# A two-layer decoder with a top-1 expert stage on one core: no fill of unused rows, five full expert blocks taken first, last logits from rows turned on TensorE, addresses loaded in groups

## What is computed

```python
x = x + local_attention(layernorm(x))                  # window of 257
x = x + perceiver_attention(ctx, layernorm(x))         # 8 heads of 128, keys = 1024 context + 512 own
x = x + bit_linear_ffn(layernorm(x))                   # int8 rows, ternary weights, conv, silu
x = x + self_attention_16_heads(layernorm(x))
x = x + rope_cross_attention_16_heads(layernorm(x), ctx)
# expert stage, over all B*S = 2048 rows
xf = layernorm(x); e = argmax(softmax(xf @ Wg + bg))   # one of NE = 8 experts per row
x = x + (gelu(xf @ W1[e] + b1[e]) @ W2[e] + b2[e])
```

## Time and profile before

| what | value |
|---|---|
| median of three runs | 2154.18 us |
| the profiled execution's own time | 2155.8 us |
| its span, first to last instruction | 2154.1 us |
| TensorE matmul busy | 1856.0 us (86%) |
| VectorE busy | 1631.2 us (76%) |
| ScalarE busy | 1281.1 us (59%) |
| GpSimd busy | 218.6 us (10%) |
| mean granted TensorE clock | 0.961 |

### The profile page before, as it was taken

How to read it: one execution, slowest core, us unless ns; L and a number is a source line. 1 busy time by engine, 2 the same in 40 slices (tenths; PEclk the granted TensorE clock), 3 DMA queues, 4 the chain that set the end, 5 groups by cost and what they waited for, 6 DMA issues and landing times.

```text
span 2154.1 us, 41917 instructions
## 1 busy us (share of the span) xinstructions
PE 1856.0 (86%) x17110; PEld 1031.9 (48%) x17110; DVE 1631.2 (76%) x2621; ACT 1281.1 (59%) x1919; POOL 218.6 (10%) x230
## 2 busy tenths in 40 slices
PE   4999988988999988988899978989899987468947
PEld 2576752324666652423666653323567663023224
DVE  8888878796888878696888768697778878339643
ACT  5666646487566656487566645668566645346912
POOL 1000001300100001300100001020100002003413
PEclk8999999999999999999999999999999999689978
DMA  7477710011477730010367640000277761942034
GB/s 273 74 126 118 133 50 12 9 46 31 82 123 126 125 65 12 9 45 21 79 121 124 115 91 12 9 26 21 62 123 124 124 117 30 127 64 101 2 88 107
DMA packets 454607, 169.51 MB, mean 79 GB/s; under 512 B 428389, under 2 KB 444016, under 8 KB 453904
## 3 DMA queue, kind: packets, MB, share of 16 engines
q1 hardware_dynamic: 449216, 149.29, 34.7%
q0 software_dynamic: 5200, 17.55, 4.9%
HBM read 45.14 MB, written 18.52 MB: 30 GB/s over the span
## 4 chain that ended last, share of the span: by engine, by line
PE 48%; DVE 27%; DMA 12%; ACT 6%; issue 4%; SPq 2%; POOL 1%; POOLq 0%; DVEq 0%; ACTq 0%
DVE nmx L2177 14%; DMA arena<-arena 11%; PE ps L753 8%; PE ps L755 8%; PE ps L754 7%; PE ps L1135 6%; PE ps L1121 3%; PE ps L925 3%; DVE arena L1987 3%; PE ps L919 2%; PE ps L920 2%; PE ps L1085 1%; ACT arena L1497 1%; PE ps L1145 1%; SPq L597 1%
## 5 line engine op out<-in xcount | busy, mean ns | idle before, releaser
L2177 DVE TENSOR_REDUCE nmx<-ps 128x2 f32<-128x1024 f32 x384 | 445.1, 1218 | 51.6 <-PE ps L1085 49.8
L1669 ACT ACTIVATE arena<-ps 128x512 f32<-128x512 f32 x768 | 406.8, 601 | 99.9 <-PE ps L1121 94.9
L1972 DVE TENSOR_SCALAR_CACHE_REDUCE ps<-ps 128x1536 f32<-128x1536 f32 x128 | 225.7, 1763 | 46.4 <-PE ps L755 45.6
L1135 PE MATMUL ps<-arena 128*17 128x256 f32 x3072 | 242.8, 393 | 0.0
L1987 DVE SCALAR_TENSOR_TENSOR arena<-arena,rs 128x1536 f16<-128x1536 f32 x128 | 231.6, 1809 | 4.2 <-ACT arena L1559 4.2
L1559 ACT ACTIVATE arena<-arena,rs 128x1536 f16<-128x1536 f32 x128 | 200.8, 1569 | 42.9 <-DVE rs L1978 42.9
L1121 PE MATMUL ps<-arena 64*128 64x512 f16 x768 | 171.0, 396 | 47.7 <-DMA arena<-arena 45.8
L1550 ACT ACTIVATE arena<-ps,nm 128x1536 f32<-128x1536 f32 x128 | 197.0, 1539 | 15.7 <-DVE ps L1972 15.7
L753 PE MATMUL ps<-arena 128*128 128x512 f16 (+2 forms) x508 | 178.5, 352 | 24.7 <-DMA arena<-zx_d 22.6
L919 PE MATMUL ps<-arena 128*128 128x128 f16 x1536 | 185.3, 219 | 0.8 <-DMA arena<-arena 0.8
L920 PE MATMUL ps<-arena 128*128 128x128 f16 x1536 | 185.3, 219 | 0.0
(11 more groups left out here) (334 smaller groups left out, 3553.7 us busy)
## 6 DMA issues: line engine op xcount, KB each, us to landing
zx_d<-in_eye POOLq DMA_DIRECT2D x7, 1300.0 KB
arena<-in_weights SPq DMA_DIRECT2D x8, 929.0 KB, 18.2
arena<-arena SPq DMA_DIRECT2D x72, 64.0 KB, 2.1
arena<-arena SPq DMA_TRANSPOSE x272, 3.7
arena<-in_ctx SPq DMA_DIRECT2D x4, 1024.0 KB, 5.5
arena<-in_ctx_t SPq DMA_DIRECT2D x4, 1024.0 KB, 4.9
arena<-in_experts SPq DMA_DIRECT2D x1, 3840.0 KB, 11.5
arena<-zx_d SPq DMA_DIRECT2D x23, 132.0 KB, 2.2
```

The costliest lines, as they stand in the source:

```text
L1135: mm(ps[32 * j:32 * j + VW, 7, cols], v17[:, kt, 4 * g_ + j, :], pr_[:, (4 * t + j) % RING, cols], start=(kt + half == 0), stop=(kt == mod ...
L1669: A(pr_[:, n % RING, :], ps[:, 4 + n % 3, :], ACT.Exp).then_inc(b_exp.sem, 1)
L1972: TS_(s_, s_, -XS, None, ALU.mult, ALU.min, accum_out=nm[:, i:i + 1]).then_inc(s_max.sem, 1)
L2177: V.tensor_reduce(nmx[:, g_ % 2, ch, :, pp, i], ps[:, 2 * (z % 2):2 * (z % 2) + 2, :], AX.X, ALU.max, negate=True)\
```

## The change

- **No fill.** `pad_regions` and its eight DMAs go. A region now is `B*S + P` = 2176 rows and begins with 128 rows of a number out of bounds, written once at the start: SyncE issues eight DMAs of 128 rows (2080 bytes each) from an SBUF tile `no_row`, ahead of the load of x for batch 0. The last block of an expert is moved back so that it ends at the expert's last row; its rows that were done by the block before are masked by `above`.
- **Five full blocks first.** `OLD = 5` blocks are certain to be full of rows of batches 0 to 2. `old_blocks` on VectorE works out their table inside the last batch's cross attention. SyncE loads them before (three) and after (two) `keep_rows`. TensorE does `block_hidden` of 0 and 1 as soon as the last x is added. `new_blocks` makes the table of the other 18 after the last routing.
- **Last logits from turned rows.** In the last batch TensorE turns `zf` with eight transposes; ScalarE and VectorE split the result into `yT`. The four DMA transposes of that batch go. `rows_lo` now comes behind `route_choice`.
- **Grouped address loads.** SyncE and TensorE load 5 and then 18 addresses each by one call, not one per block.
- **Aligned base.** The buffer `arena` is the first in SBUF, and weight slices take a constant offset first and the register second. Block tables lie over `rope_k`. Two semaphore steps replace a wait of VectorE on itself in `finish_block`.

```diff
-PAD = (NE - 1) * P
-REGION = (B - 1) * S + PAD
+OLD = (B - 1) * S // P - (NE - 1)
+REGION = B * S + P
...
+        ARENA = 96 * 1024 + 512
+        arena = sb("arena", [P, ARENA // 4])
         wh, wl = sb("wh", [P, NW], F16), sb("wl", [P, NW], F16)
...
             sp.wait_ge(w_lo.sem, WCH)
             sp.wait_ge(pad_out.sem, 16)
+            sp.wait_ge(pads_set.sem, 15)
+            for e in range(NE):
+                sp.dma_start(zx_d[REGION * e:REGION * e + P, :], no_row).then_inc(pad_out.sem, 16)
...
-                keep_rows(b)
-            transpose_rows(B - 1)
-            sp.wait_ge(zx_out.sem, zx_out.at(B, 16 * NE))
-            sp.wait_ge(e_table.sem, e_table.at(0, 1))
-            for j in range(NB):
+                if b < B - 1:
+                    keep_rows(b)
+            def rows_at(j0, j1):
+                return nc.values_load_multi_w_load_instructions(where[0:1, 1, j0:j1], engines=(mybir.EngineType.SP,),
+                                                                min_val=0, max_val=NE * REGION - P)[1]
+            def load_block(j, at):
                 r_ = j % BR
-                at = sp.value_load(where[0:1, 1, j:j + 1], min_val=0, max_val=NE * REGION - P)
                 if j >= BR:
                     sp.wait_ge(e_h.sem, e_h.at(0, 2 * (j - BR)) + 2)
                     sp.wait_ge(o_out[r_].sem, 16 * (j // BR))
                 rows = zx_d[bass.ds(at, P), :]
                 sp.dma_start_transpose(zb[r_], rows[:, 0:D].bitcast(F16)).then_inc(block_in[r_].sem, 16)
                 sp.dma_start(xb[r_], rows[:, D:ZW]).then_inc(block_in[r_].sem, 16)
+            sp.wait_ge(e_table.sem, e_table.at(0, 1))
+            old = rows_at(0, OLD)
+            sp.wait_ge(zx_out.sem, zx_out.at(B - 1, 0))
+            sp.wait_ge(pad_out.sem, 16 * (1 + NE))
+            sp.wait_ge(pv_mm.sem, pv_mm.at(B - 1, 8 * 48))
+            for j in range(OLD - 2):
+                load_block(j, old[j])
+            keep_rows(B - 1)
+            for j in range(OLD - 2, OLD):
+                load_block(j, old[j])
+            sp.wait_ge(e_table.sem, e_table.at(0, 4))
+            new = rows_at(OLD, NB)
+            sp.wait_ge(zx_out.sem, zx_out.at(B, 0))
+            for j in range(OLD, NB):
+                load_block(j, new[j - OLD])
...
-                        if b == B - 1:
-                            pad_regions()
...
-                scatter_rows(b)
-            for j in range(NB):
+                if b < B - 1:
+                    scatter_rows(b)
+            for j in range(2):
+                scatter_block(j)
+            scatter_rows(B - 1)
+            for j in range(2, NB):
                 scatter_block(j)
...
+            def transpose_last():
+                for i in range(NT):
+                    pe.wait_ge(y_ready.sem, y_ready.at(B - 1, Y_FIRST[6] + i + 1))
+                    for c in range(DC):
+                        last = nc.tensor.transpose(ps[:, LAST_BANK[c], P * i:P * i + P], zf[:, i, P * c:P * c + P], ident[:])
+                        if i == NT - 1:
+                            last.then_inc(n_t.sem, 1)
...
-                                   [(tuple(ewc[:, bass.ds(at + (HE * part + D * c + P * m), P)] for part in range(2)),
+                                   [(tuple(ewc[:, HE * part + D * c + P * m:][:, bass.ds(at, P)] for part in range(2)),
...
             def experts():
+                pe.wait_ge(ew_lo.sem, 2 * NE)
+                pe.wait_ge(e_table.sem, e_table.at(0, 3))
+                at = list(weights_at(0, OLD))
+                pe.wait_ge(lx_added.sem, lx_added.at(B - 1, 2 * NT))
+                for j in range(2):
+                    block_hidden(j, at[j])
+                transpose_last()
+                for j in range(2):
+                    block_out(j, at[j])
                 route_logits(B - 1)
+                block_hidden(2, at[2])
                 route_ranks(B - 1)
+                for j in range(3, OLD):
+                    block_hidden(j, at[j])
+                    block_out(j - 1, at[j - 1])
+                pe.wait_ge(e_table.sem, e_table.at(0, 4))
+                at += weights_at(OLD, NB)
+                pe.wait_ge(e_table.sem, e_table.at(0, 6))
+                for j in range(OLD, NB + 1):
                     if j < NB:
-                        at[j] = block_hidden(j)
-                    if j:
-                        block_out(j - 1, at[j - 1])
+                        block_hidden(j, at[j])
+                    block_out(j - 1, at[j - 1])
...
+                    if m_ == 1 and b == B - 1 and t == mode.last_shift // 2:
+                        old_blocks()
...
@@ the stream of VectorE @@
             def experts():
                 normalise(B - 1, 4, x, zf)
+                for j in range(2):
+                    split_block(j)
+                for c in range(DC):
+                    dve.wait_ge(n_hi.sem, n_hi.at(B, c + 1))
+                    TT(yT[1][:, c, :], ps[:, LAST_BANK[c], :], yT[0][:, c, :], ALU.subtract).then_inc(n_lo.sem, 1)
+                for j in range(2):
+                    finish_block(j)
+                route_choice(B - 1)
                 rows_lo(B - 1)
-                route_choice(B - 1)
                 route_slots(B - 1)
-                block_tables()
-                for j in range(NB + 1):
+                new_blocks()
+                for j in range(2, NB + 1):
```

More of the change, by code:

```diff
@@ L155, in decoder @@
         slot = sb("slot", [P, NT], U32)
-        pad_at = b2[0:1, 0:NE].bitcast(I32)
         st = sb("st", [P, NT, 6])
@@ L216, in decoder @@
         caff_first = Layout(81920).take([4, S])
+        no_row = Layout(92160).take([ZW])
+        b2 = Layout(95232).take([D])[0:NE]
         xn = Layout().take([NT, D])
-        zTt = [Layout(32768 if b == B - 1 else 4096).take([4 * NT, P], F16) for b in range(B)]
+        zTt = Layout(4096).take([4 * NT, P], F16)
         zf = Layout(77824).take([NT, D])
@@ L1554, in scaled_hi @@
                 act.wait_ge(s_rs.sem, s_rs.at(b, n + 1))
-                if b and n < 2:
-                    act.wait_ge(zx_out.sem, zx_out.at(b, 0))
+                if n < 2:
+                    act.wait_ge(*((zx_out.sem, zx_out.at(b, 0)) if b else (pad_out.sem, 16 * (1 + NE))))
                 if turn is not None:
@@ L2359, in across, with count_rows @@
                 return v_.unsqueeze(1).to_broadcast([P, n, v_.shape[-1]])
[L2361 to L2367 removed]
+            blocks, ends, skip, many = (cnt[:, k] for k in range(4))
+            def count_rows():
                 own.link(STT(many, count_up[:, 0:NE], -1.0 * REGION, held[:], ALU.mult, ALU.add))
+                own.link(TS_(many, many, -1.0 * P, None, ALU.add))
@@ new lines, in running, with table, along, chosen @@
+            def running(dst, src):
+                own.link(TT(bt[:, 0, 0:NE], upto, across(src, NE), ALU.mult))
+                own.link(V.tensor_reduce(dst, bt[:, 0, 0:NE], AX.X, ALU.add))
+            def table(j0, j1, sizes, whole):
+                n = j1 - j0
+                owner, first, past, start = (bs[:, k, 0:n] for k in range(4))
+                is_past, one = bt[:, 0, 0:n], bt[:, 1, 0:n]
+                def along(v_):
+                    return v_.unsqueeze(2).to_broadcast([P, n, NE])
+                def chosen(dst, values):
+                    own.link(TT(bt[:, 2, 0:n], one, across(values, n), ALU.mult))
+                    own.link(V.tensor_reduce(dst, bt[:, 2, 0:n], AX.X, ALU.add))
+                own.link(TT(is_past, along(count_up[:, 0:n]), across(ends, n), ALU.is_ge))
+                own.mark(V.tensor_reduce(owner, is_past, AX.X, ALU.add))
+                own.link(TT(bt[:, 2, 0:n], is_past, across(sizes, n), ALU.mult))
+                own.link(V.tensor_reduce(first, bt[:, 2, 0:n], AX.X, ALU.add))
+                own.mark(TS_(where[:, 0, j0:j1], owner, NE - 1.0, 2.0 * EW, ALU.min, ALU.mult))
+                own.mark(TT(one, along(owner), across(count_up[:, 0:NE], n), ALU.is_equal))
+                own.link(TT(past, count_up[:, 1:n + 1], first, ALU.subtract))
+                if whole:
+                    own.link(TS_(start, past, 1.0 * P, None, ALU.mult))
+                else:
+                    chosen(first, skip)
+                    own.link(TT(past, past, first, ALU.add))
+                    chosen(first, many)
+                    own.link(STT(start, past, 1.0 * P, first, ALU.mult, ALU.min))
+                    own.link(TS_(owner, owner, NE - 1.0, None, ALU.min))
+                own.link(STT(start, owner, 1.0 * REGION, start, ALU.mult, ALU.add))
+                V.tensor_copy(where[:, 1, j0:j1], start).then_inc(e_table.sem, 1)
+                b1_ = col[:, COL["b1"]:COL["b1"] + NE * DC].rearrange("p (e m) -> p m e", m=DC)
+                for m in range(DC):
+                    own.mark(TT(pick1[:, 0:n, m, :], one, across(b1_[:, m, :], n), ALU.mult))
+                own.wait()
+                V.tensor_reduce(bias1[:, j0:j1], pick1[:, 0:n], AX.X, ALU.add).then_inc(e_table.sem, 1)
```

(18 more changed lines are left out.)

171 lines of the change are left out of this document (83 added, 88 removed).

## The result

The changed kernel takes 2081.88 us (median of four, 2077.21 to 2085.14); the kernel before took 2152.61 beside it. The ratio is 0.9669, 95% interval 0.9643 to 0.9696: faster. The forecast was 2084.

The account below looks back on a forecast made before the run. Batch 3's self attention was bound by DMA engines full of fill rows, with the expert stage second. -49.5 - 22.1 + 1.0 = -70.6 gave a span of 2083.5 and a forecast of 2084 us, range 2072 to 2102.

Parts of the forecast that it names:

- The fill goes: Self attention of batch 3: without the fill's 11.2 MB it takes the pace of batch 2, saving 49.5 us (46 to 50).
- the rival that the fill was not the cause: Batch 3: the 49.5 us come from something else, only the tail moves, 2133 us; chance 0.03.
- Its replacement: Start of the kernel: eight DMAs ahead of x of batch 0 cost +1.0 us, bounds 0 and 12.4.
- the rival with 12.4 us: Start: the eight writes go at the fill's rate, VectorE stands 12.4 us waiting for x, total 2095; chance 0.12.
- The ring order: Start: each DMA engine consumes descriptors in ring order, so x would not overtake the eight writes, 2.13 MB.
- old_blocks: VectorE behind the last shift split: 28 small instructions, 6.2 us, fit in an idle 8.36 us; cost 0, bounds 0 to 1.
- The head of the routing: Start of the expert stage: last logits from turned rows start the choice 5.0 us earlier and the slots 3.6 us earlier.
- Grouped loads: SyncE before block 5: loading 18 addresses costs 5 us, between hidden under the scatters and 10; block 5 loaded at 2077.3.
- a sign of being wrong: Expert stage: more than 6 us between the table and block 5's transpose would show the forecast wrong.
- The pace: Last 18 blocks: six buffers set 2.3 us a block, bounds 2.04 to 2.76; seventeen steps take 39.1 us.
- The tail: Expert stage to the end: ends at 2131.95, 22.1 us earlier than 2154.1; bounds 9.2 to 30.6 us.
- The moved buffer: All arena tiles change address: put at 0; rival of slower engine accesses in all batches, 2192 us at 5%, chance 0.02.

## Why the prediction was right, step by step

- **The fill goes, -49.5.** Measured -50.2. Both runs with the fill put back show that it was its traffic, which rules out the rival that the fill was not the cause; and the choice of batch 2's pace over the sum of the waits (61.7) was the right one.
- **Its replacement, +1.0.** The first use of x moved by 1.2 us; the rival with 12.4 us is ruled out. The eight writes stood ahead of x and x was still late by 0.53 us only. Of the 1.2 us, 0.53 are that wait, and 0.35 are the moved subtraction of b2, which the term did not have; and with x first the next instruction began no earlier. So the 1.0 came out right partly for another reason.
- **The ring order** that I cited from the Trainium skill (DMA: Bandwidth & Descriptors, Queues, rings and completion order) fits these two traces: x took 4.6 us to land behind the writes, 3.8 in the kernel before, and is not waited for when it is first. The two traces do not prove it, since a sharing of the engines between x and the writes would look alike.
- **old_blocks, 0.** Right: VectorE's next instruction still waits for TensorE, 3.37 us where the earlier trace rows had 8.36.
- **The head of the routing, slots 3.6 us earlier.** 5.5 us: mis-sized. `block_hidden` of 0 and 1 ended before zf was complete, so that TensorE's eight transposes (1.04 us) and the choice came 1.3 us sooner than I had reckoned; the rest is that `rows_lo`, which I had added in full, in part filled VectorE's wait for TensorE's counts.
- **Grouped loads, 5 us.** This is the step that failed: 9.2 us from table to transpose, near the upper bound of 10 and beyond the 6 us that I had named as a sign of being wrong. Rather more than half of the 4.2 us was made up for in the head, as the table was there 13.0 us behind zf and not 15.3: block 5 was loaded 1.8 us later than forecast. The 18 registers alone took 4.05 us, 0.2 + 0.21 for each, and each check 0.25 us beside it. The Trainium skill's figure of about 200 ns a register even in bulk (Runtime: NRT & Kernel Launch, Instruction fetch mechanics) agrees with this trace for that load, though the page gives it for loads from HBM and these read SBUF; I had set it aside by putting loads and checks together at 5. A grouped load saved little or nothing per address here (0.21 to 0.23 us a register for 0.28 alone); it moved the whole price ahead of block 5. And I had not put TensorE's own load on the path at all. It adds 1.5 us behind SyncE's, and the run with SyncE's addresses one by one shows that it alone holds block 5 back as long.
- **The pace, 2.3.** 2.46 in one profile and 2.34 in the other of the same kernel. At 2.46 it is 2.7 us too short over seventeen steps. The runs with seven buffers, 2.18 and 2.23 (2.33 with the load of a second group in it) where seven profiles with six buffers and grouped loads have 2.34 to 2.49, speak for the round over the six buffers, as argued; the faster loads there changed as well.
- **The tail, -22.1.** -17.7 in the first profile, 1.8 short by the head and 2.7 by the pace; in the second, whose tail is 75.8, -21.3.
- **The moved buffer, 0.** The rival that it slows the engines is ruled out: the 1811.5 us ahead of batch 3's split are no longer than before, and the engines' busy times are within 7 us.
- **The sum** came out at -70.8 for -70.6, closer than its terms: the tail was 4.4 us short, and the 2.8 us that lie ahead of batch 3's split, which no step of the change explains, made up for most of it. The right sum is in part luck; that it is within some 5 us is not.

## What to carry to other kernels

Compare the same stage over the loop's rounds before anything else: a stage that is 50 us longer in one round names its cause by what else happens there, and the other rounds give the price of removing it. Bulk DMA traffic, even from an idle engine to a tensor nobody waits for, is paid by each small DMA that is on the path, here with a wait of some 16 us and 13 us of the stage for each, and moving it to another stage of that kind only moves the bill. Loading addresses in a group was not cheaper by itself here: ask what stands behind the whole group, leave out range checks that the table already guarantees, and look at every engine that loads, since relieving one of two gained nothing. Whether a small first group helps is left open by these runs.

## What the hardware showed that I had not expected

The same load of 18 registers took 4.05 us in the changed kernel and 1.79 us with seven buffers, where one more word ahead of the table moved its base by 4 bytes; on TensorE 4.42 and 1.61 us. The line view of the seven-buffer kernel:

```profile
L596 SPq TENSOR_LOAD <-rope_k x2: 1283/1539/1795, 1978.6 to 2019.6; - x2
...
L1401 PEldq TENSOR_LOAD <-rope_k x2: 1430/1520/1611, 2001.0 to 2024.0; - x2
```

The smaller loads of five registers stayed at 1.28 us, and in the kernel with two groups a load of three took 1.05 and one of fifteen 3.26. So the price per register was about 0.21 us in some places and 0.09 in others. That the alignment of the first word decides it is my inference; the base alone was not varied. 2.2 us of the seven-buffer kernel's shorter head come from this and not from the buffers. Left open as well is the spread of the tail between executions of one kernel, 75.8 and 79.5 us. The granted clock does not explain it by itself: between 2030 and 2040 us it was 0.63 in the execution with the longer tail and 0.59 in the one with the shorter.
